# Scale rows and softmax-sum rows through DRAM, and negated maxima by ScalarE, in a two-layer contextual attention kernel

## The chip, the core and the metric

One core of one Trainium2 chip runs the whole kernel. The metric is the device time of one execution in microseconds, the median of several runs. Five engines work from queues of their own and meet by semaphores: TensorE (PE; PEld are its weight loads), VectorE (DVE), ScalarE (ACT), GpSimd (POOL) and SyncE (SP), which here only issues transfers.

## The reference

Two layers of the same operation on `b` of 4 images x 64 channels x 80 x 80. All masks are zero, so `mm` is 1. Per image:

```python
f = b[:, :, ::2, ::2]                                # 40 x 40
w = patches(f, 3, stride=1)                          # 1600 patches of 64*3*3
raw_w = patches(b, 4, stride=2)                      # 1600 patches of 64*4*4
norm = sqrt(sum(w * w))                              # one per patch
wn = w / maximum(norm, 1e-4)
yi = einsum('bpd,bld->blp', w, wn) * mm              # l scaled by its norm
yi = softmax(yi * 10, axis=1) * mm                   # over l, for each position p
out = einsum('blp,bld->bpd', yi, raw_w)              # then overlap-add of the 4x4 patches, / 4
```

The scores before scaling are symmetric in `p` and `l`; the scale belongs to one side, the softmax sum to the other.

## The kernel before

A unit is one image in one layer: 8 units. The 1600 positions are 14 tiles of 123 partitions (`TW`, 3 strips of 41). The score matrix `G` stays in SBUF, tile `t` in partitions, all positions along the free side. It is walked in four chunks of columns of 2, 4, 4 and 4 tiles for scores (`S_CHUNKS`) and 4, 4, 4 and 2 for the second half (`P_CHUNKS`), each in 7 pairs of tiles: 28 pairs, one per slot.

One loop body (L339, L526, L736, L1004, one for each engine) has 28 slots, `s` = 2 to 29. Three units are in flight in it: `u` is in its second half (softmax and products), `v` in its scores, `w` is being loaded. The order within a slot is written out by hand and is the same on all engines. First body (None, 0, 1), then six of (u, u+1, u+2), one without `w`, and a last one with `u` alone.

Scores of a pair: TensorE makes products of shifted feature tiles in `psG` (L465), or transposes blocks of `G` that exist already (L475); ScalarE copies them to `G` (L656, L672), VectorE adds a third row (L860). `maxima` (L886) multiplies a tile of `G` with the scale row `RB` and reduces the maximum to `mx`; `negate` (L902) writes `nm = -mx`; ScalarE's `score_sums` (L685) takes `Exp` with bias `nm` and accumulates the sum `sg`. In slots 23, 24, 28 and 29 four chunk sums become `lse`, in two parts: tiles 0 to 3, then the rest.

Second half of a pair: `argument_pair` (L960, VectorE, four slots ahead) computes `G * RA - lse row`; `softmax_pair` (L701, ScalarE) takes `Exp`; SyncE's `shift_pair` (L317) moves the result one partition on, SBUF to SBUF, in two transfers of 112 and of 10 rows (`SHIFT_PARTS`), to `SH`; `add_shifted` (L972, two slots ahead) adds it; `sum_pair` (L981, one slot ahead) makes `Z`, at the start of a chunk with the strip `SHJ` from `shift_strip` (L328); `paste_tile` (L509, TensorE) multiplies `Z` with the image blocks `B` into `psO`, and `read_out` (L710, ScalarE, slots 7, 14, 21, 28) copies `psO` to `OSB`, which `store_chunk` (L309) writes to DRAM.

Two vectors with one value per position are needed as rows, the same in all 123 partitions: the scale (`RB`) and `lse`. Both are made as columns, position in the partition. `spread` (L404) makes a row from a column: a transpose on TensorE whose input is one column, broadcast to 123 columns. Scale rows take 14 transposes per unit in four groups, in slots 25 and 26 (groups 0 and 1, of the unit to come), 4 (group 2) and 18 (group 3, two tiles), each followed by a ScalarE copy to `RB` (L633). Softmax rows take 14 in four chunks, in slots 24, 2, 5 and 10 (the last with two tiles); VectorE reads them in PSUM bank `k % 2` of `psB`.

SyncE's queue takes in order, per slot: feature loads (3 transfers, slot 3), image loads (6, slot 9), `shift_pair`, `shift_strip`, feature layout (slots 10 to 12), `store_chunk` (slots 8, 15, 22 and 29). It waits in front of each.

Of the kernel before, what the change touches and what calls it, by code (L numbers as in the profile page):

```python
# [28 lines left out]
NK = len(P_CHUNKS)  # L29
SLOTS = NK * PAIRS  # L30
# [11 lines left out]
FIRST = 2  # L42
# [38 lines left out]
def contextual_attention(nc, x, mask0, mask1, ident, valid, out):  # L81
    mid = nc.dram_tensor("mid", (IMAGES, C, SIDE, SIDE), F32, kind="Internal").ap()

    with ExitStack() as ctx:
# [19 lines left out]
        SQ = sb("SQ", [128, FROWS // 2 * TW], F32)  # L104
        RB = sb("RB", [TW, TILES * TW], F32)
# [22 lines left out]
        R = sb("R", [TW, TILES], F32)  # L128
# [35 lines left out]
        r_rows = sem("r_rows")  # L164
        norm_cols = sem("norm_cols")
# [33 lines left out]
        R_STEPS = 10  # L199
# [8 lines left out]

        ROW_BANK = [psB[0:TW, 1, :], psB[0:TW, 1, :], psM[0:TW, :], psB[0:TW, 0, :]]

# [52 lines left out]
        def _(sp):  # L263
# [119 lines left out]
        def _(pe):  # L383
# [4 lines left out]
            def row_squares(v, w):  # L388
                pe.wait_ge(sq_made, (w + 1) * SQ_STEPS)
                pe.sem_inc(pe_gate, 1)  # L390
                if v is not None:

                    pe.wait_ge(r_rows, v * 4 + 3)
# [16 lines left out]
            def scale_rows(u, v, g):  # L410

                pe.wait_ge(r_step, (v + 1) * R_STEPS)
                if u is not None:
                    pe.sem_inc(pe_gate, 1)
                    if g == 2:
                        pe.wait_ge(b_made, (u + 1) * PAIRS)
                    else:
                        pe.wait_ge(arg_made, u * NB + (3 if g == 3 else NK) * TILES)
                if g == 1:
                    pe.sem_inc(pe_gate, 1)  # L420
                    pe.wait_ge(r_rows, v * 4 + 1)
                spread(ROW_BANK[g], R, 4 * g, min(4 * g + 4, TILES)).then_inc(r_psum, 1)

            def lse_row(v, w, k):
# [3 lines left out]
                if k == 0:  # L428
                    pe.wait_ge(r_rows, v * 4 + 4)
                elif k == 1 and w is not None:  # L430
                    pe.wait_ge(r_rows, w * 4 + 2)
                else:
                    pe.wait_ge(arg_made, v * NB + (k - 1) * TILES)
                s0, n = P_CHUNKS[k]
                spread(psB[0:TW, k % 2, :], lse, s0, s0 + n).then_inc(lse_rows, 1)

            def block_group(v, w, g):
                if g == 0:
                    pe.wait_ge(image_in, (v + 1) * 6 * 16)
                    pe.sem_inc(pe_gate, 1)  # L440

                if g:
                    pe.wait_ge(b_made, v * PAIRS + g)
                elif w is not None:
                    pe.wait_ge(r_step, w * R_STEPS + 4)
                else:
                    pe.wait_ge(r_rows, v * 4 + 3)
# [78 lines left out]
            def body(u, v, w):  # L526
                for s in BODY:
                    at = place(u, v, s)
                    pairs = score_list(s) if v is not None else []
                    if s == 4 and v is not None:  # L530
                        scale_rows(u, v, 2)
                    if s == 18 and v is not None:
                        scale_rows(u, v, 3)
                    if s == 5 and u is not None:
                        lse_row(u, v, 2)
                    if s == 10 and u is not None:
                        lse_row(u, v, 3)
# [13 lines left out]
                    if s == FIRST and u is not None:  # L551
                        lse_row(u, v, 1)
# [8 lines left out]
                    if s == 24 and v is not None:  # L561
                        lse_row(v, w, 0)
# [24 lines left out]
            scale_rows(None, 0, 0)  # L587
            scale_rows(None, 0, 1)
# [7 lines left out]
        def _(act):  # L596
# [36 lines left out]
            def scale_rows(v, g):  # L633
                act.wait_ge(r_psum, v * 4 + g + 1)
                n = min(4, TILES - 4 * g) * TW
                act.activation(RB[:, 4 * g * TW:4 * g * TW + n], ROW_BANK[g][:, 0:n], ACT.Copy).then_inc(r_rows, 1)
# [99 lines left out]
            def body(u, v, w):  # L736
                for s in BODY:
# [29 lines left out]
                    if s == 4 and v is not None:  # L767
                        scale_rows(v, 2)
                    if s == 18 and v is not None:
                        scale_rows(v, 3)  # L770
                    if w is not None:
                        if s == 5:
                            high_features(w)
                        if s == 6:
                            squares(w)
                        if s == 12:
                            roots(w)
                        if s in (25, 26):
                            scale_rows(w, s - 25)
# [14 lines left out]
            scale_rows(0, 0)  # L794
            scale_rows(0, 1)
# [9 lines left out]
        def _(dve):  # L805
# [31 lines left out]
            def scales(v, w):  # L837
# [10 lines left out]
                if v is not None:  # L848

                    dve.sem_inc(dve_gate, 1)  # L850
                    dve.wait_ge(r_rows, (v + 1) * 4)
                mm = mm20[:, bass.ds(w * TILES, TILES)]
                dve.tensor_tensor(R[:, :], rcp[:, :], mm, ALU.mult).then_inc(r_step, 1)
# [32 lines left out]
            def maxima(v, j, par):  # L886
# [3 lines left out]
                if i == 0 and par == 0 and k != 1:  # L890
                    dve.wait_ge(r_rows, v * 4 + max(k + 1, 2))
                    dve.sem_inc(dve_gate, 1)
# [9 lines left out]
            def negate(v, j):  # L902
                dve.wait_ge(max_made, v * NB + 2 * j + 2)
                c = j // PAIRS * TILES + 2 * (j % PAIRS)
                dve.tensor_scalar(nm[:, c:c + 2], mx[:, 2 * (j % 2):2 * (j % 2) + 2], -1.0, None,  # L905
                                  ALU.mult).then_inc(neg_made, 1)

            def score_pair(v, j):

                add_third_row(v, j, 0)  # L910
                if j - 1 not in (-1, 22):
                    maxima(v, j - 1, 1)
                    negate(v, j - 1)
                add_third_row(v, j, 1)
                maxima(v, j, 0)
                if j in (22, SLOTS - 1):

                    maxima(v, j, 1)
                    negate(v, j)
# [40 lines left out]
            def argument_pair(at):  # L960
                u, k, i = at
                c0, n = p_cols(k)
                if i == 0:
                    dve.wait_ge(lse_rows, u * NK + k + 1)
                    dve.sem_inc(dve_gate, 1)
                for t in arg_tiles(i):
                    g = G[:, t * GLEN + c0:t * GLEN + c0 + n]
                    dve.scalar_tensor_tensor(out=g, in0=g, scalar=RA[:, bass.ds(u * TILES + t, 1)],  # L968
                                             in1=psB[0:TW, k % 2, 0:n],
# [34 lines left out]
            def body(u, v, w):  # L1004
                for s in BODY:
# [26 lines left out]
                    if w is not None:  # L1032
# [6 lines left out]
                        if s == 20:  # L1039
                            scales(v, w)  # L1040
# [41 lines left out]
            scales(None, 0)  # L1082
# [62 lines left out]
```

## Time and profile before

| | us |
|---|---|
| median of three runs | 1434.59 (1431.02 to 1434.99) |
| the profiled execution | 1435.39 |
| its span, first to last instruction | 1433.6 |

```profile
PEld 4756765676556665577656676567655766566433
DVE 3667889799888898889897888979987898978983
ACT 2677646676557565586565764666655855658331
```

The three lines show the span in 40 equal slices, each digit the busy share in tenths. A unit's period of about 170 us is 4.7 slices: VectorE and ScalarE are fullest together where the scores of one unit end and the second half of it begins.

```profile
L697 ACT ACTIVATE S<-S,nm 123x480 f32<-123x480 f32 (+3 forms) x560 | 308.5, 555 | 161.2 <-DVE nm L905 160.8
L968 DVE SCALAR_TENSOR_TENSOR G<-G,RA,psB 123x492 f32<-123x492 f32 (+1 forms) x448 | 270.4, 647 | 0.0
```

A group's line has: line, engine, operation, output <- inputs, shapes, count | busy us, mean ns of one | idle time of the engine in front of them, and what ended most of it.

### The profile page before, as it was taken

What the parts mean: (1) busy time and instruction counts of PE and PEld (TensorE: products, weight loads), DVE (VectorE), ACT (ScalarE), POOL (GpSimd) and SP (SyncE); (2) the same over time, 40 slices, a digit from 0 to 9 for tenths busy, and PEclk for the clock granted to TensorE, in tenths of its full rate; (3) what the DMA queues carried; (4) which work ended last, traced back from release to release, by engine and by line L of the source; (5) the groups of instructions that cost most, each with busy time, mean ns of one, the idle gap of its engine ahead of it and who ended that gap; (6) DMA issues with size and microseconds to landing.
All of it is one profiled execution on the core that took longest, in us unless ns stands there. A gap on an engine that the chain in (4) does not pass through costs nothing.

```text
span 1433.6 us, 24384 instructions
## 1 busy us (share of the span) xinstructions
PE 1327.2 (93%) x7190; PEld 894.6 (62%) x7190; DVE 1183.3 (83%) x2827; ACT 857.9 (60%) x2233; POOL 46.9 (3%) x62
## 2 busy tenths in 40 slices
PE   4988999999999899999999899999999999998886
PEld 4756765676556665577656676567655766566433
DVE  3667889799888898889897888979987898978983
ACT  2677646676557565586565764666655855658331
POOL 1000000010000100001000000001000010000100
PEclk9997999999999999999999999999999999999998
DMA  5502482145822556135741359224572236313442
GB/s 91 89 1 85 109 173 76 47 116 119 163 64 67 124 113 150 49 86 127 143 117 33 104 118 179 70 52 110 126 156 67 71 107 135 94 32 96 131 136 53
DMA packets 180471, 142.54 MB, mean 99 GB/s; under 512 B 119859, under 2 KB 177267, under 8 KB 180339
## 3 DMA queue, kind: packets, MB, share of 16 engines
q1 hardware_dynamic: 180178, 140.50, 41.7%
q8 instruction: 57, 0.93, 0.3%
q10 hardware_dynamic: 160, 0.49, 0.2%
q14 instruction: 76, 0.61, 0.1%
HBM read 19.76 MB, written 13.11 MB: 23 GB/s over the span
## 4 chain that ended last, share of the span: by engine, by line
PE 54%; DVE 15%; ACT 11%; issue 8%; SPq 7%; DMA 5%; DVEq 0%; POOL 0%; ACTq 0%; POOLq 0%
PE psO L521 26%; PE psG L471 23%; SPq L326 4%; DVE G L968 4%; ACT S L697 4%; DVE Z L1001 3%; DMA SH<-G 3%; PE psG L480 3%; DVE S L898 3%; ACT G L708 2%; ACT G L683 2%; DVE G L979 2%; DMA SHJ<-G 2%; SPq L270 1%; ACT SQ L624 1%
## 5 line engine op out<-in xcount | busy, mean ns | idle before, releaser
L521 PE MATMUL psO<-Z,B 123*128 123x492 f32 (+2 forms) x1792 | 718.6, 530 | 46.0 <-DVE Z L1001 31.4
L521 PEld LDWEIGHTS psO<-Z,B 123*128 123x128 f32 x1792 | 325.8, 194 | 247.6 <-issue 133.8
L471 PE MATMUL psG<-LH,HL 128*123 128x246 f16 (+2 forms) x2616 | 407.2, 285 | 3.7 <-ACT G L670 3.0
L697 ACT ACTIVATE S<-S,nm 123x480 f32<-123x480 f32 (+3 forms) x560 | 308.5, 555 | 161.2 <-DVE nm L905 160.8
L471 PEld LDWEIGHTS psG<-LH,HL 128*123 128x123 f16 x2616 | 277.4, 137 | 125.4 <-issue 64.5
L708 ACT ACTIVATE G<-G,nb 123x492 f32<-123x492 f32 (+1 forms) x448 | 265.0, 639 | 60.3 <-DVE G L968 59.9
L898 DVE CUSTOM_DVE_ANT_0 S<-G,RB 123x492 f32<-123x492 f32 (+1 forms) x448 | 268.4, 604 | 25.8 <-ACT G L683 15.6
L979 DVE TENSOR_TENSOR G<-G,SH 123x492 f32<-123x492 f32 (+1 forms) x448 | 247.6, 591 | 48.9 <-DMA SH<-G 48.3
L968 DVE SCALAR_TENSOR_TENSOR G<-G,RA,psB 123x492 f32<-123x492 f32 (+1 forms) x448 | 270.4, 647 | 0.0
L883 DVE TENSOR_TENSOR G<-G,psG 123x492 f32<-123x492 f32 (+2 forms) x272 | 135.0, 496 | 90.4 <-PE psG L471 46.5
L1001 DVE TENSOR_TENSOR Z<-G 123x984 f32<-123x984 f32 (+2 forms) x192 | 197.2, 1028 | 0.0
L471 PE MATMUL psG<-H 128*123 128x123 f16 (+3 forms) x872 | 193.8, 284 | 0.0
L683 ACT ACTIVATE G<-psG 123x492 f32<-123x492 f32 (+3 forms) x256 | 119.7, 471 | 117.0 <-PE psG L471 76.3
L670 ACT ACTIVATE G<-psG 123x246 f32<-123x246 f32 (+1 forms) x136 | 63.6, 468 | 115.5 <-PE psG L471 115.2
L480 PEld LDWEIGHTS psG<-idn,G 123*123 123x123 f32 x672 | 95.4, 190 | 59.0 <-issue 22.4
L480 PE MATMUL psG<-idn,G 123*123 123x123 f32 x672 | 108.5, 281 | 17.9 <-ACT G L683 13.2
L471 PEld LDWEIGHTS psG<-H 128*123 128x123 f16 x872 | 102.7, 137 | 21.0 <-issue 0.4
L471 PE MATMUL psG<-HL 128*123 128x492 f16 (+2 forms) x392 | 111.8, 285 | 0.0
L697 ACT ACTIVATION_READ_ACCUMULATOR S<-S,nm 123x1 f32 x560 | 106.7, 191 | 0.0
L1109 POOL COPY G<-G 123x246 f32<-123x246 f32 x56 | 42.9, 774 | 1292.4 <-DVE mx L898 1162.5
L717 ACT ACTIVATE OSB<-psO 128x492 f32<-128x492 f32 (+2 forms) x64 | 31.4, 548 | 78.8 <-PE psO L521 78.7
L471 PE MATMUL psG<-HV 128*123 128x246 f16 (+2 forms) x240 | 67.7, 282 | 0.0
(79 smaller groups left out, 575.8 us busy)
## 6 DMA issues: line engine op xcount, KB each, us to landing
SH<-G SPq DMA_DIRECT2D x336, 214.8 KB
SH<-G SPq DMA_DIRECT2D x112, 89.2 KB
SH<-G SPq DMA_DIRECT2D x336, 19.2 KB
XP<-x SPq DMA_DIRECT2D x20, 280.0 KB, 5.7
XP<-mid SPq DMA_DIRECT2D x20, 280.0 KB, 5.5
HL<-LH SPq DMA_DIRECT2D x16, 246.5 KB, 4.5
mid<-OSB SPq DMA_DIRECT2D x48, 80.0 KB, 2.3
out<-OSB SPq DMA_DIRECT2D x48, 80.0 KB, 2.3
```

What stands on the lines that cost most here:

```text
L471: last = pe.matmul(psG[0:TW, bank, b0 * TW:b1 * TW], st[:, v % 2, p:p + TW], mv[:, v % 2, lo:lo + n], start=i == 0, stop=i == len(terms) - 1)
L480: last = pe.transpose(psG[0:TW, par, i * TW:(i + 1) * TW], G[:, c:c + TW], idn[0:TW, 0:TW])
L521: last = pe.matmul(psO[:, b, 0:n], B[:, o:o + 128], Z[:, 2 * (s % 2) + j, 0:n], start=t == 0, stop=t == TILES - 1)
L670: act.activation(to, psG[0:TW, FREE, stored * TW:w * TW], ACT.Copy).then_inc(p_copied, 1)
L683: act.activation(G[:, c:c + n], psG[0:TW, par, 0:n], ACT.Copy).then_inc(part if shared else read, 1)
L697: last = act.activation(y, y, ACT.Exp, bias=nm[:, k * TILES + t:k * TILES + t + 1], accum_out=sg[:, c:c + 1])
L708: act.activation(y, y, ACT.Exp, bias=nb[:, bass.ds(u * TILES + t, 1)]).then_inc(y_made, 1)
L883: dve.tensor_tensor((odd if par else even)[:, b0 * TW:n], rows[:, p0 * TW:p0 * TW + n - b0 * TW], psG[0:TW, par, b0 * TW:n], ALU.add).then ...
L898: dve.tensor_tensor_reduce(S[:, slot, 0:n], tile_of(j, 2 * i + par)[:, 0:n], RB[:, s0 * TW:s0 * TW + n], 1.0, 0.0, ALU.mult, ALU.max, mx[: ...
L968: dve.scalar_tensor_tensor(out=g, in0=g, scalar=RA[:, bass.ds(u * TILES + t, 1)], in1=psB[0:TW, k % 2, 0:n], op0=ALU.mult, op1=ALU.subtrac ...
L979: dve.tensor_tensor(g, g, SH[:, o % SFREE, 0:n], ALU.add).then_inc(y1_made, 1)
L1001: dve.tensor_tensor(Z[:, slot:slot + 2, 0:n], g[:, 2 * i:2 * i + 2, c0:c0 + n], g[:, 2 * i - 1:2 * i + 1, c0 - TW:c0 - TW + n], ALU.add).t ...
```

## The change

1. Scales. Of unit 0, groups 0 and 1 are still made by `spread`. Otherwise one transpose per unit (`turn_scales`, slot 22) turns the 14 columns of `RA` into 14 rows of 123, ScalarE copies them (slot 23), SyncE writes them to DRAM (slot 24) and loads them back, broadcast to 123 partitions, one load per score chunk: slots 26 and 28 for the next unit's chunks 0 and 1, slots 4 and 10 for chunks 2 and 3. The column vector `R` goes; `RA` held the same.
2. Softmax sums. Rows of chunks 0 and 1 are made as before, each in a PSUM bank of its own. The last six tiles (chunks 2 and 3) are turned by one transpose (slot 2), copied by ScalarE (slot 2), written (slot 3) and loaded, broadcast, into `LB` (slot 5). VectorE's arguments of chunks 2 and 3 read `LB`.
3. `negate` runs on ScalarE, in front of the exponentials of its pair; that of pair 22 at the start of slot 23.

Waits are set to match. The core of the diff:

```diff
+RFIRST = 8
+LHEAD = 8
+LTAIL = TILES - LHEAD
...
+            def write_scales(w):
+                sp.wait_ge(scales_copied, w + 1)
+                sp.dma_start(scale_row[w].rearrange("(t p) -> t p", p=TW), RT[:, :]).then_inc(scales_out, 16)
+            def load_scales(w, k):
+                t0, n = S_CHUNKS[k]
+                if w == 0:
+                    if t0 + n <= RFIRST:
+                        return
+                    n, t0 = t0 + n - max(t0, RFIRST), max(t0, RFIRST)
+                else:
+                    sp.wait_ge(max_made, (w - 1) * NB + (k + 1) * TILES)
+                    sp.sem_inc(sp_gate, 1)
+                sp.wait_ge(scales_out, (w + 1) * 16)
+                row = scale_row[w:w + 1, t0 * TW:(t0 + n) * TW]
+                sp.dma_start(RB[:, t0 * TW:(t0 + n) * TW], row.to_broadcast([TW, n * TW])).then_inc(scales_in[k], 16)
+            def write_lse(u):
+                sp.wait_ge(lse_copied, u + 1)
+                sp.dma_start(lse_tail[u].rearrange("(t p) -> t p", p=TW), LT[:, :]).then_inc(lse_out, 16)
+            def load_lse(u):
+                sp.wait_ge(arg_made, u * NB)
+                sp.sem_inc(sp_gate, 1)
+                sp.wait_ge(lse_out, (u + 1) * 16)
+                sp.dma_start(LB[:, :], lse_tail[u:u + 1, :].to_broadcast([TW, LTAIL * TW])).then_inc(lse_in, 16)
...
+                    if s == FIRST and u is None:
+                        write_scales(v)
+                    if s == 3 and u is not None:
+                        write_lse(u)
+                    if s == 5 and u is not None:
+                        load_lse(u)
+                    if s in (4, 10) and v is not None:
+                        load_scales(v, 2 if s == 4 else 3)
+                    if s == 24 and w is not None:
+                        write_scales(w)
+                    if s in (26, 28) and w is not None:
+                        load_scales(w, 0 if s == 26 else 1)
...
+            def turn_scales(u, w):
...
+                pe.transpose(psB[0:TILES, 1, 0:TW], RA[:, w * TILES:(w + 1) * TILES],
+                             idn[0:TW, 0:TW]).then_inc(scales_turned, 1)
+            def turn_lse(v, u):
...
+                pe.transpose(psM[0:LTAIL, 0:TW], lse[:, LHEAD:TILES], idn[0:TW, 0:TW]).then_inc(lse_turned, 1)
...
-                    if s == 4 and v is not None:
-                        scale_rows(u, v, 2)
-                    if s == 18 and v is not None:
-                        scale_rows(u, v, 3)
-                    if s == 5 and u is not None:
-                        lse_row(u, v, 2)
-                    if s == 10 and u is not None:
-                        lse_row(u, v, 3)
...
-                        lse_row(u, v, 1)
+                        lse_row(u, 1)
+                        turn_lse(v, u)
...
+                    if s == 22 and w is not None:
+                        turn_scales(u, w)
...
-                    if w is not None and s in (25, 26):
-                        scale_rows(u, w, s - 25)
...
+                act.activation(RT[:, :], psB[0:TILES, 1, 0:TW], ACT.Copy).then_inc(scales_copied, 1)
...
+                act.activation(LT[:, :], psM[0:LTAIL, 0:TW], ACT.Copy).then_inc(lse_copied, 1)
...
+            def negate(v, j):
+                act.wait_ge(max_made, v * NB + 2 * j + 2)
+                c = j // PAIRS * TILES + 2 * (j % PAIRS)
+                act.activation(nm[:, c:c + 2], mx[:, 2 * (j % 2):2 * (j % 2) + 2], ACT.Copy,
+                               scale=-1.0).then_inc(neg_made, 1)
             def score_sums(v, j):
                 k, i = j // PAIRS, j % PAIRS
+                if j != 22:
+                    negate(v, j)
...
+                    if s == 23 and v is not None:
+                        negate(v, 22)
...
+                row = psB[0:TW, k, 0:n] if k < 2 else LB[:, c0 - LHEAD * TW:c0 - LHEAD * TW + n]
```

## Rows read from the trace of the kernel before

**Rows 1.** Page, busy time of each engine (us, share of the span, instructions).
```profile
PE 1327.2 (93%) x7190; PEld 894.6 (62%) x7190; DVE 1183.3 (83%) x2827; ACT 857.9 (60%) x2233; POOL 46.9 (3%) x62
```
**Rows 2.** Page, chain of waits, shares of the span by engine.
```profile
PE 54%; DVE 15%; ACT 11%; issue 8%; SPq 7%; DMA 5%; DVEq 0%; POOL 0%; ACTq 0%; POOLq 0%
```
**Rows 3.** List of waits, whole span: waiting us in total, times, longest.
```profile
ACT S L697 <- DVE nm L905: 160.8, 120, 4.1
...
DVE G L979 <- DMA SH<-G: 48.3, 26, 4.8
...
PE psO L521 <- DVE Z L1001: 31.4, 17, 4.6
...
PE psO L521 <- ACT OSB L717: 4.8, 6, 1.9
```
**Rows 4.** Windows of one steady unit: us, busy of each engine (instructions), clock, DMA share, GB/s.
```profile
666.40:672.40 6.00, 6.00 (x50) 4.86 (x48) 4.74 (x13) 3.63 (x10) 0.03 (x1) 1.00 1.01 218
682.00:773.00 91.00, 89.41 (x407) 53.80 (x408) 78.39 (x178) 48.46 (x119) 0.00 (x0) 1.00 0.49 109
773.00:818.00 45.00, 40.60 (x237) 30.24 (x236) 38.73 (x106) 38.34 (x116) 1.65 (x3) 1.00 0.27 73
```
**Rows 5.** Chain in order of time, TensorE, 682 to 698 us: start, us, what.
```profile
682.25 3.54 PE psO L521 x8
...
697.76 0.21 PE psB L406 x2
```
**Rows 6.** Groups by form, VectorE: count, busy us, mean ns, idle before.
```profile
L979 DVE TENSOR_TENSOR G<-G,SH 123x492 f32<-123x492 f32 x336 | 210.8, 665 | 41.5 <-DMA SH<-G 40.9
...
L883 DVE TENSOR_TENSOR G<-G,psG 123x492 f32<-123x492 f32 x128 | 85.3, 667 | 42.3 <-PE psG L471 39.7 <-ACT G L670 2.7
...
L905 DVE TENSOR_SCALAR nm<-mx 123x2 f32<-123x2 f32 x224 | 38.0, 169 | 7.8
```
**Rows 7.** Timeline of VectorE, 793 to 801 us: start, us, engine, line, operation.
```profile
793.54 0.08 DVE L898 DVE_READ_ACCUMULATOR2_ANT mx<- 123x1 f32 x1
...
793.93 0.67 DVE L898 CUSTOM_DVE_ANT_0 S<-G,RB 123x492 f32<-123x492 f32 x1
...
799.96 0.08 DVE L898 DVE_READ_ACCUMULATOR2_ANT mx<- 123x1 f32 x1
799.96 1.36 DVE L968 SCALAR_TENSOR_TENSOR G<-G,RA,psB 123x492 f32<-123x492 f32 x2
```
**Rows 8.** Timeline of ScalarE, 23 and 788 us.
```profile
23.24 0.22 ACT L629 ACTIVATE lnn<-nsq 123x14 f32<-123x14 f32 x1 [6.88 <-DVE nsq L835]
23.49 0.21 ACT L631 ACTIVATE root<-lnn 123x14 f32<-123x14 f32 x1
...
788.40 0.22 ACT L729 ACTIVATE ed<-df 123x16 f32<-123x16 f32 x1
788.51 0.56 ACT L697 ACTIVATE S<-S,nm 123x320 f32<-123x320 f32 x1
```
**Rows 9.** Timeline of SyncE's queue, 661 to 675 us.
```profile
661.74 2.07 SPq L270 DMA_DIRECT2D XP<-mid  x3
663.91 9.65 SPq L326 DMA_DIRECT2D SH<-G  x12
673.69 1.22 SPq L337 DMA_DIRECT2D SHJ<-G  x2
```
**Rows 10.** Timeline of VectorE, 670 to 679 us, with its idle time and what ended it.
```profile
670.05 0.67 DVE L979 TENSOR_TENSOR G<-G,SH 123x492 f32<-123x492 f32 x1 [0.95 <-DMA SH<-G]
...
677.65 0.67 DVE L997 TENSOR_TENSOR Z<-G,SHJ 123x492 f32<-123x492 f32 x1 [1.14 <-DMA SHJ<-G]
678.24 0.66 DVE L998 TENSOR_TENSOR Z<-G 123x492 f32<-123x492 f32 x1
```
**Rows 11.** DMA issues: count, KB each, median us to landing.
```profile
HL<-LH SPq DMA_DIRECT2D x16, 246.5 KB, 4.5
...
out<-OSB SPq DMA_DIRECT2D x8, 20.0 KB, 1.9
```

More of the change, by code:

```diff
@@ L82, in contextual_attention @@
     mid = nc.dram_tensor("mid", (IMAGES, C, SIDE, SIDE), F32, kind="Internal").ap()
+    scale_row = nc.dram_tensor("scale_row", (UNITS, TILES * TW), F32, kind="Internal").ap()
+    lse_tail = nc.dram_tensor("lse_tail", (UNITS, LTAIL * TW), F32, kind="Internal").ap()
     with ExitStack() as ctx:
@@ L104, in contextual_attention @@
         SQ = sb("SQ", [128, FROWS // 2 * TW], F32)
+        RT = sb("RT", [TILES, TW], F32)
+        LT = sb("LT", [LTAIL, TW], F32)
+        LB = sb("LB", [TW, LTAIL * TW], F32)
         RB = sb("RB", [TW, TILES * TW], F32)
@@ L164, in contextual_attention @@
         r_rows = sem("r_rows")
+        scales_turned = sem("scales_turned")
+        scales_copied = sem("scales_copied")
+        scales_out = sem("scales_out")
+        scales_in = [sem(f"scales_in{k}") for k in range(NK)]
+        lse_turned = sem("lse_turned")
+        lse_copied = sem("lse_copied")
+        lse_out = sem("lse_out")
+        lse_in = sem("lse_in")
         norm_cols = sem("norm_cols")
@@ L390, in row_squares @@
                 pe.sem_inc(pe_gate, 1)
-                if v is not None:
-                    pe.wait_ge(r_rows, v * 4 + 3)
+                if v:
+                    pe.wait_ge(b_made, v * PAIRS)
                 for r in range(FROWS // 2):
@@ L424, in lse_row, with scale_rows @@
-            def lse_row(v, w, k):
+            def scale_rows(g):
+                pe.wait_ge(r_step, R_STEPS)
+                spread(psB[0:TW, g, :], RA, 4 * g, 4 * g + 4).then_inc(r_psum, 1)
+            def turn_scales(u, w):
+                pe.wait_ge(r_step, (w + 1) * R_STEPS)
+                pe.sem_inc(pe_gate, 1)
+                if u is not None:
+                    pe.wait_ge(arg_made, u * NB + 2 * TILES)
+                else:
+                    pe.wait_ge(r_rows, 2)
+                pe.transpose(psB[0:TILES, 1, 0:TW], RA[:, w * TILES:(w + 1) * TILES],
+                             idn[0:TW, 0:TW]).then_inc(scales_turned, 1)
@@ L426, in lse_row @@
+            def turn_lse(v, u):
+                pe.wait_ge(lse_dve, (u + 1) * LSE_STEPS)
+                pe.sem_inc(pe_gate, 1)
+                pe.wait_ge(b_made, (u + 1) * PAIRS)
+                pe.transpose(psM[0:LTAIL, 0:TW], lse[:, LHEAD:TILES], idn[0:TW, 0:TW]).then_inc(lse_turned, 1)
+            def lse_row(v, k):
                 pe.wait_ge(lse_dve, v * LSE_STEPS + (LSE_STEPS // 2 if k == 0 else LSE_STEPS))
                 pe.sem_inc(pe_gate, 1)
[L428 to L431, printed above, removed]
+                if k == 1:
+                    pe.wait_ge(scales_copied, min(v + 2, UNITS))
+                elif v == 0:
+                    pe.wait_ge(r_rows, 1)
@@ L432, in lse_row @@
                 else:
-                    pe.wait_ge(arg_made, v * NB + (k - 1) * TILES)
+                    pe.wait_ge(arg_made, (v - 1) * NB + (k + 1) * TILES)
                 s0, n = P_CHUNKS[k]
-                spread(psB[0:TW, k % 2, :], lse, s0, s0 + n).then_inc(lse_rows, 1)
+                spread(psB[0:TW, k, :], lse, s0, s0 + n).then_inc(lse_rows, 1)
             def block_group(v, w, g):
@@ L445, in block_group @@
                     pe.wait_ge(r_step, w * R_STEPS + 4)
[L446 to L447 removed]
+                elif v:
+                    pe.wait_ge(b_made, v * PAIRS)
                 for t in (2 * g, 2 * g + 1):
@@ L586, in _ @@
             band_sums(None, 0)
-            scale_rows(None, 0, 0)
-            scale_rows(None, 0, 1)
+            scale_rows(0)
+            scale_rows(1)
+            turn_scales(None, 0)
             body(None, 0, 1)
@@ L766, in body @@
                         softmax_pair(at)
[L767 to L770, printed above, removed]
+                    if s == FIRST and u is not None:
+                        copy_lse(u)
                     if w is not None:
@@ L793, in _ @@
             roots(0)
-            scale_rows(0, 0)
-            scale_rows(0, 1)
+            scale_rows(0)
+            scale_rows(1)
+            copy_scales(0)
             act.wait_ge(mask_ready, 1)
@@ L835, in squared_norms, with scales @@
                 dve.tensor_scalar(nsq[:, :], psM[0:TW, 0:TILES], 1e-8, None, ALU.max).then_inc(r_step, 1)
-            def scales(v, w):
+            def scales(w):
                 at = w * R_STEPS
@@ L889, in maxima @@
                 n = w * TW
-                if i == 0 and par == 0 and k != 1:
-                    dve.wait_ge(r_rows, v * 4 + max(k + 1, 2))
+                if i == 0 and par == 0:
+                    if k < 2 and v == 0:
+                        dve.wait_ge(r_rows, 2)
+                    else:
+                        dve.wait_ge(scales_in[k], (v + k // 2) * 16)
                     dve.sem_inc(dve_gate, 1)
@@ L968, in argument_pair @@
                     dve.scalar_tensor_tensor(out=g, in0=g, scalar=RA[:, bass.ds(u * TILES + t, 1)],
-                                             in1=psB[0:TW, k % 2, 0:n],
+                                             in1=row,
                                              op0=ALU.mult, op1=ALU.subtract).then_inc(arg_made, 1)
@@ L1039, in body @@
                         if s == 20:
-                            scales(v, w)
+                            scales(w)
             dve.wait_ge(mask_step, 1)
@@ L1081, in _ @@
             squared_norms(0)
-            scales(None, 0)
+            scales(0)
             body(None, 0, 1)
```

54 lines of the change are left out of this document (21 added, 33 removed).

## The prediction

> **What bounds the kernel now.** I read the busy shares of the page first: TensorE is busy for 93% of the span, VectorE 83%, ScalarE 60% [rows 1]. Alone that says "take work off TensorE", and the change takes 136 small transposes off it. So I read the chain of waits next: only 54% of it is TensorE's; 15% is VectorE, 11% ScalarE, 7% SyncE's queue and 5% transfers [rows 2]. The reader is to see that the bound changes hands. The list of waits says where: TensorE waits 31.4 us for VectorE's sums `Z` and 4.8 us for the output copies, ScalarE 160.8 us for the negated maxima `nm`, VectorE 48.3 us for shift transfers [rows 3]. Last I cut one steady unit (654 to 824 us, a period of 170 us) into windows [rows 4] and walked the chain through it. Three stages come out.
>
> Stage one, 654 to 682 us (slots 2 to 7): TensorE is full, but a second path ends almost together with it. SyncE issues nearly without a break from 654 to 673 (store, shifts, three feature loads, shifts) [rows 9], the 16 DMA engines are saturated in 666 to 672 [rows 4], VectorE waits 0.95 us for a shift and later 1.14 us for the strip `SHJ` [rows 10], and the stage ends when ScalarE, after features and squares, has copied `OSB`: TensorE starts again at 682.25 [rows 5].
>
> Stage two, 682 to 773 us (slots 7 to 20): TensorE is busy 89.4 of 91 us [rows 4]. What leaves TensorE here counts in full.
>
> Stage three, 773 to 818 us (slots 21 to 29): ScalarE is busy 38.3 and VectorE 38.7 of 45 us [rows 4]; the chain runs on ScalarE from 781 to 790, then on VectorE until 817, where TensorE takes up a sum `Z` that it has waited for (17 such waits, up to 4.6 us [rows 3]).
>
> **The change, part by part.**
>
> *Transposes gone from TensorE.* One column-to-row transpose is 0.21 us / 2 = 0.105 us of the chain [rows 5]. A unit had 28; now it has 8 (softmax rows of chunks 0 and 1) plus two single ones that turn 14 and 6 columns at once. In stage two go those of chunk 3 in slot 10 and of scale group 3 in slot 18, 4 together: 0.42 us, off the path that ends the stage. Seven bodies have both: 2.9 us. In stage one go 8 and come 1: 0.74 us, in stage three go 8 and come 1; both lie beside the other paths.
>
> *Negation moved.* VectorE: 224 instructions of 169 ns [rows 6]. What one is worth depends on what follows. From the end-read of one maximum to the next maximum it takes 0.39 us (793.54 to 793.93), and with no negation between, the next instruction starts with the read itself (799.96) [rows 7]. So 0.39 before a maximum; before an argument I take 0.19, the instruction and its start, and before an add 0.35, an estimate between the two, nearer to the first because an add has gates to pass as a maximum has. On the path of stage three lie two of the first kind, one of the second and one of the third: -1.32 us. ScalarE: a small instruction whose result the next one needs costs 23.49 - 23.24 = 0.25 us; one that nothing right behind it needs, 788.51 - 788.40 = 0.11 us [rows 8]. Where the exponentials already waited for `nm` (most of the 160.8 us) it costs nothing: 0.17 + 0.04 us of VectorE is replaced by 0.21 + 0.04 of ScalarE. It costs in the unbroken ScalarE run 781 to 790: pairs 20 and 21 at 0.25, pair 22 (taken out in front) at 0.11: +0.61 us, which VectorE's sum of slot 23 waits for. Stage three: +0.61 - 1.32 = -0.71 us.
>
> *Row copies on ScalarE.* Four copies per unit go, two of 14x123 and 6x123 come. None of those gone lies in the run 781 to 790; they cover part of the other negations. I take 0.
>
> *Rows from SBUF in place of PSUM for the arguments of chunks 2 and 3.* The trace has no such instruction before. An add with a PSUM operand takes 667 ns, one without 665 ns [rows 6]: I take 0, bounds 0.06 us either way for each of 28 tiles. The Trainium skill (VectorE: DVE Perf Modes, The TRN2 errata) gives a fixed 58 cycles for SBUF sources against 120 for PSUM; by that the 28 instructions would save 1.8 us of VectorE a unit, most of it in stage two where VectorE is not the bound. The two rows above speak against it.
>
> *Seven more issues on SyncE.* Each takes about 0.7 us of its queue (three feature loads: 2.07 us [rows 9]). Order matters. The write of the scales (slot 24) and the loads of slots 26 and 28 fall in gaps, though the last one ends just when the shift of slot 29 wants the queue: +0.1 us at the head of SyncE's unbroken stretch. The write in slot 3 comes behind that slot's shifts, so the shift for which VectorE waits 0.95 us isn't touched. But it and the load of slot 4 push the shifts of slot 5 and the strip (issued 673.69 [rows 9]) back: 1.3 us less some 0.8 us for which SyncE stood idle in that row of twelve issues, 0.5 us. VectorE's sum ended at 678.9 and TensorE used it at 682.25, 3.3 us later [rows 10, 5]: covered. If the strip came over 3 us later, or the sum after it over 1 us, all beyond is lost. The loads of slots 5 and 10 and of the last unit's row are needed five or more slots on. No instruction of VectorE should wait for a row. Write and load together are two transfers of 2 to 4.5 us [rows 11] against 12 us between their slots.
>
> *What survives stage one.* It starts 0.71 us earlier and TensorE has 0.74 us less in it, but SyncE's stretch starts 0.1 us later, and in units where ScalarE's run to `OSB` starts right behind TensorE one negation adds 0.25. If SyncE's path decides everywhere, nothing survives; if TensorE's does, 1.2 us. TensorE has six waits at `OSB`, from nearly nothing to 1.9 us [rows 3], so both happen. I take 0.3 us, near the lower end, since a path that was second becomes first.
>
> *The sum.* Seven bodies of -0.42 - 0.3 = -5.0. First body (no shifts yet; the chain is TensorE, then ScalarE, then VectorE; two removed copies and 14 removed transposes lie on it, and +0.61 as above): -2.0, bounds -4 and +1. Last body, where VectorE and SyncE are the chain and have two issues more: +0.7, bounds 0 and +3. Together -6.3 us. The profiled execution took 1435.39 us (span 1433.6), 0.8 above the median of 1434.59; 1434.6 - 6.3 = 1428.3. I say **1428.5**.
>
> **The rivals.**
>
> *A, stage one eats it (no change).* SyncE's queue and the strip are the path in every unit, ScalarE's added 0.25 falls before `OSB`, and only the 0.42 of stage two stays, against +0.7 at the end and perhaps a short spell at the lower clock more: -2.9 + 0.7 + 0.7 = -1.5: 1433. For it: the saturated 666 to 672 and both waits in rows 10. Against: the waits there are about 1 us.
>
> *B, all of it counts (faster).* -0.42 - 1.2 a unit, and -3 at the start: -14: 1420. For it: TensorE's 93%. Against: rows 2 and 10.
>
> *C, the broadcast loads crowd out the shifts (slower).* Place: slots 4 and 5. Each load writes 123 rows of 1968 bytes (2952 for the softmax row), 242 and 363 KB. A load of 246.5 KB lands after 4.5 us, one of 20 KB after 1.9 [rows 11], so 2.6 us is moving when it is spread well. If few of the 16 engines carry it, they move the same bytes for several times 2.6 us, and the strip and shifts behind it wait for just those engines. The kernel cuts its shifts into 112 and 10 rows, so that most rows are a multiple of 16; the loads aren't cut. It decides from the point at which the strip lands over 1 us later than now (the smallest cover of the sum behind it). On 3 of 16 engines it would be 13.9 us at the moving rate of that row, of which about 4 pass before the strip is issued and 4 are covered: up to +6 a unit. That row's time holds queueing, so the lower bound is 0. I price it at +2 us a unit in seven units, with +3 at the end: 1428.5 + 14 + 3 = 1445. The Trainium skill (DMA: Bandwidth & Descriptors, Why a DMA increments its semaphore by 16 and not by 1) says that a transfer uses the largest number of engines up to 16 that divides its slowest dimension; for 123 rows that is 3. No row of before shows how many engines a transfer used.
>
> **How the numbers follow.** Forecast 0.42, A 0.22, B 0.13, C 0.23. This kernel's runs tell 0.3% (4.3 us) from no change, so faster is below 1430.3, slower above 1438.9. Faster: 0.7 of the forecast's 0.42, B, and a fifth of A: 0.29 + 0.13 + 0.04 = 0.46. Slower: nearly all of C, 0.21, and 0.01 of the rest: 0.22. Same: 0.32. Range 1419 to 1442: it takes in B and A and the lower half of C. The forecast's own range is 1424 to 1432.
>
> **What would show it.** Right: 4 transposes less per unit between the `OSB` copies of slots 7 and 21, with that stretch 0.4 us shorter; from that copy to TensorE's restart in slot 29 about 0.7 us less; TensorE's wait at `OSB` in slot 7 grown from 0.8 to about 2 us (so part is lost there). ScalarE's new negation near 0.2 us, VectorE's waits for rows 0. C would show as waits of VectorE for `SHJ` or `SH` well over the 48.3 us of rows 3, and as a bigger wait of TensorE for `Z` in slots 8 to 13. B would show no wait at `OSB`. It would be wrong if ScalarE's run in stage three grew by more than 1.3 us, or if SyncE stood waiting for a DRAM write with shifts queued behind it.

## The result

The changed kernel is slower: 1443.81 us median of 6 runs (1441.28 to 1445.91), against 1431.27 us for the kernel before, run beside it. The ratio is 1.0087, 95% interval [1.0064, 1.011]. The forecast was 1428.5 us, range 1419 to 1442, so the sign was wrong. Rival C had the sign, part of the place and, with 1445 us, nearly the time.

The profiled execution took 1445.91 us (span 1444.1), at the granted clock of before (0.983 both). Busy times and the shares of the chain of waits, from the page of after; they answer to [rows 1] and [rows 2]:

```profile
PE 1317.9 (91%) x7054; PEld 875.8 (61%) x7054; DVE 1138.6 (79%) x2595; ACT 888.5 (62%) x2443; POOL 46.8 (3%) x62
...
PE 32%; DVE 18%; SPq 14%; ACT 13%; issue 11%; DMA 10%; DVEq 0%; POOL 0%; ACTq 0%; POOLq 0%
```

The work went as the diff says: TensorE 136 instructions less, VectorE 44.7 us less. Yet the span grew by 10.5 us: TensorE's idle time (span less busy time) went from 106.4 to 126.2 us, and SyncE's queue and the transfers went from 12% of the chain to 24%. The list of waits, answering to [rows 3] (waiting us, times, longest):

```profile
ACT nm L763 <- DVE mx L981: 169.1, 116, 4.6
...
DVE G L1058 <- DMA SH<-G: 63.3, 44, 4.8
...
DVE Z L1076 <- DMA SHJ<-G: 42.4, 29, 4.2
...
PE psO L588 <- DVE Z L1080: 24.5, 17, 3.0
...
PE psG L538 <- DVE G L963: 15.6, 14, 2.3
...
PE psO L588 <- ACT OSB L800: 5.5, 5, 1.7
```

The second and third rows show what happens to VectorE: it waits 15.0 us more for shifts than in [rows 3], and 42.4 us for strips, which had been

```profile
DVE Z L997 <- DMA SHJ<-G: 18.7, 20, 3.9
```

before. The fifth row is what TensorE sees of it: it waits for adds that VectorE makes late, for which it had waited

```profile
PE psG L471 <- DVE G L883: 0.2, 1, 0.2
```

before. These waits are no measure of the loss by themselves: below stand kernels with nearly as much of them and no loss. No line has VectorE waiting for `RB` or `LB`: the new rows come in time, their neighbours don't.

Two stretches of one unit show how. SyncE's queue at the start of stage one, first of before, then of after (start, us, queue, line, transfer, count):

```profile
823.06 3.90 SPq L314 DMA_DIRECT2D mid<-OSB  x6
827.06 2.83 SPq L326 DMA_DIRECT2D SH<-G  x4
830.02 2.07 SPq L270 DMA_DIRECT2D XP<-mid  x3
```
```profile
824.00 0.36 SPq L371 DMA_DIRECT2D RB<-scale_row  x1
824.45 2.81 SPq L342 DMA_DIRECT2D SH<-G  x4
827.32 5.59 SPq L330 DMA_DIRECT2D mid<-OSB  x6
833.02 2.84 SPq L342 DMA_DIRECT2D SH<-G  x4
835.99 1.36 SPq L286 DMA_DIRECT2D XP<-mid  x2
```

Six stores take 5.59 us to issue in place of 3.90: behind the load of slot 28 the second one alone held SyncE for 2.31 us. Only part of that belongs to the three engines, as the first experiment shows. The packet records have that load's 123 rows moving from 825.0 to 830.1, three at a time. And two windows of after (window, us, busy of PE, PEld, DVE, ACT and POOL, granted clock, DMA share, GB/s):

```profile
851.00:852.00 1.00, 1.00 (x8) 0.70 (x6) 0.53 (x1) 0.97 (x3) 0.00 (x0) 1.00 0.20 77
853.00:854.00 1.00, 0.69 (x7) 0.46 (x5) 0.96 (x2) 0.97 (x4) 0.00 (x0) 1.00 0.20 80
```

A share of 0.20 is 3 of 16 engines (0.19). In the second rows of `LB` move alone; they start at 852.45. In the first, what moves is nearly all of one kind: the last 37 rows of a shift (1964 bytes each), issued behind the load of slot 4. The share says that the other engines move nothing: the shift ends on three engines. The last 17 rows of the strip's size, up to 852.4, go the same way. The timeline of VectorE in this unit (the bracket is its idle time and what ended it), answering to [rows 10]:

```profile
844.28 0.67 DVE L1058 TENSOR_TENSOR G<-G,SH 123x492 f32<-123x492 f32 x1 [1.80 <-DMA SH<-G]
...
846.28 0.67 DVE L1058 TENSOR_TENSOR G<-G,SH 123x492 f32<-123x492 f32 x1 [1.34 <-DMA SH<-G]
...
853.04 0.67 DVE L1076 TENSOR_TENSOR Z<-G,SHJ 123x492 f32<-123x492 f32 x1 [1.51 <-DMA SHJ<-G]
```

### The profile page after: what moved, and what is told of

It reads as the page before. It is cut to its first block, busy times and chain, and to the rows that moved or that the text cites. A ratio compares the mean times of both kernels' runs of the same rounds, so it can differ in the third digit from the quotient of the medians.

```text
span 1444.1 us, 24161 instructions
## 1 busy us (share of the span) xinstructions
PE 1317.9 (91%) x7054; PEld 875.8 (61%) x7054; DVE 1138.6 (79%) x2595; ACT 888.5 (62%) x2443; POOL 46.8 (3%) x62
## 4 chain that ended last, share of the span: by engine, by line
PE 32%; DVE 18%; SPq 14%; ACT 13%; issue 11%; DMA 10%; DVEq 0%; POOL 0%; ACTq 0%; POOLq 0%
PE psO L588 15%; PE psG L538 15%; SPq L342 8%; DMA SH<-G 6%; DVE G L1047 5%; ACT S L780 5%; DMA SHJ<-G 4%; DVE Z L1080 4%; ACT G L791 3%; SPq L286 3%; SPq L330 2%; DVE G L963 2%; ACT G L758 2%; DVE S L981 2%; DVE G L1058 2%
## 5 line engine op out<-in xcount | busy, mean ns | idle before, releaser
L1047 DVE SCALAR_TENSOR_TENSOR G<-G,RA,psB 123x492 f32<-123x492 f32 x224 | 151.6, 722 | 0.2
L763 ACT ACTIVATE nm<-mx 123x2 f32<-123x2 f32 x224 | 44.9, 200 | 169.9 <-DVE mx L981 169.1
L1047 DVE SCALAR_TENSOR_TENSOR G<-G,RA,LB 123x492 f32<-123x492 f32 (+1 forms) x224 | 120.1, 579 | 0.0
```

## The experiments

Each ratio is to the kernel before, run on the same chip. Intervals are of 95%. Where the time went I read from the start of TensorE's first product on `Z` in slots 2, 8 and 21 of each unit. The table has the difference to before (us) in one profiled execution each: "start" is up to slot 2 of unit 1, the stages are sums over units 1 to 6, "tail" is the rest.

```
kernel                     ratio    start  one    two    three  tail    low 1  low 3
e5  negation on ScalarE    1.0007   -0.1   +4.7   -0.4   -5.8   -1.2      3.4    3.4
after                      1.0087   -0.5   +9.9   +3.6   -4.3   +1.8      0.0   13.7
e1  loads of 128 rows      1.0007   -3.9   +13.2  -2.8   -5.7   +2.0     13.7    6.8
e10 loads of 126 rows      1.0016   -4.2   +7.9   -2.5   -6.3   -1.5      6.8    6.8
e9  loads of 127 rows      1.1089   +18.3  +68.7  +60.4  -8.8   +10.8    54.6    0.0
e2  negation on VectorE    1.0112   -1.5   +3.8   +7.9   -2.4   +1.6      0.0   13.7
e3  slot 28 of 128 rows    1.0043   -4.4   +8.6   +1.4   -6.1   +2.9      0.0    6.8
e6  slot 28 of 123 rows    1.0045   -4.8   +9.7   -3.3   -4.3   +1.5      6.8   10.2
e15 e1, loads twice        1.0003   -3.5   +7.4   -2.2   -5.7   +0.8      0.0   10.2
e7  128 rows, moved        0.9983   -3.9   +3.9   -2.4   -3.1   +1.6      3.4   10.2
e11 as e7, VectorE negates 0.9982   +1.2   -4.1   -2.6   +0.4   +1.9      0.0   17.1
e8  123 rows, moved        1.0198   -0.4   +4.5   +19.2  -6.6   +1.7      3.4    6.8
```

The last two columns are the time in stages one and three at TensorE's lower clock (1.2 GHz, granted 0.50); the kernel before has 0.0 and 17.1. Stage two repeats well between kernels. Stages one and three don't, since these spells stand at other places in each execution. A profiled execution isn't the median either: that of before took 1435.4 us, 4 above its median beside after, that of e1 was the slowest of its twelve (1438.2, median 1431.6), that of e10 stood 4.6 and that of e8 6.2 below theirs.

**The number of engines.** e1, all loads of 128 rows into tiles of 128 partitions:

```
-LB = sb("LB", [TW, LTAIL * TW], F32)
+LB = sb("LB", [128, LTAIL * TW], F32)
...
-row.to_broadcast([TW, n * TW])
+row.to_broadcast([128, n * TW])
```

> The changed kernel with both broadcast tiles of 128 partitions and loads of 128 rows in place of 123 (4% more bytes, the same number and place of transfers). Theory F (few engines: a load of 123 rows runs on 3 of the 16 DMA engines, and the stores, shifts and strip behind it wait for those three): the loss goes. VectorE's waits for SH and SHJ come back from 106 to about 70 us, no store issue stalls (2.3 us in slot 29), and the time falls by 10 to 16 us, to 0.995 to 1.000 of before. Theory I (seven more issues on SyncE, or simply 9 MB more bytes): nothing changes by more than 3 us, 1.008. Theory N (negation on ScalarE): nothing changes either, 1.008.

1431.64 us, 1.0007 [0.9991, 1.0024]. The whole loss goes, with 4% more bytes loaded. The strip's line is back at

```profile
DVE Z L1076 <- DMA SHJ<-G: 19.9, 22, 3.9
```

and 128 rows of `LB` move in 2.3 us, up to 15 at a time, where 123 rows took 5.2, three at a time. One thing was expected and didn't come: that no issue of a store stalls. The six stores above take 4.66 us in e1 (the longest 1.38). In the mean of the slot 29 stores of six bodies they take 4.19 us in before, 5.21 in after and 4.60 in e1, so 0.6 of the 1.0 us a unit is the three engines'. The other cause on trial, the negation (e2, back on VectorE in the changed kernel; e5, moved to ScalarE in the kernel before):

> The changed kernel with the sign change back on VectorE, loads of 123 rows as they were. Theory N: the loss goes, 1.000. Theories F and I: VectorE loses its gain of about 0.7 us a unit in slots 21 to 29 while the waits for shifts stay, so the time is the same or 2 to 5 us more: 1.008 to 1.012.

> The kernel before with nothing but the sign change moved to ScalarE. Theory N: slower by 8 to 12 us, 1.007. Theory F and my own sum (stage three -0.7 us a unit, part of it lost in slot 7): -1 to -4 us, 0.997 to 0.999.

e2: 1448.17 us, 1.0112 [1.0082, 1.0142]. e5: 1432.7 us, 1.0007 [0.9994, 1.002], so the gain expected of it (0.997 to 0.999) isn't there either. The negation isn't the loss. Two more kernels ask how the engines are chosen, with 126 and with 127 in place of 128:

> The change with loads of 126 rows. If the number of engines is the largest number up to 16 that divides the rows, 126 gives 14 engines: ratio 1.000 to 1.002, like the loads of 128 rows (1.0007), landing in some 4 us. Rival: only whole multiples of 16 rows are spread over all engines and any other number falls to few: ratio 1.006 or more.

> The change with loads of 127 rows, a prime. By the same rule one engine carries the whole load: 127 rows one after another at 82 to 118 ns each make 10 to 15 us a load against 3.4 to 5 us with three engines, the scale and softmax rows come late or hold one engine's share of shifts and strips: ratio 1.02 to 1.05, DMA share 0.06 in a stretch with such a load alone. Rival (the rows are spread by size and not by divisors): ratio 1.000 to 1.002, as with 128.

126 rows: 1433.38 us, 1.0016 [0.9997, 1.0035]. 127 rows: 1587.99 us, 1.1089 [1.1069, 1.1108], worse than I had expected. TensorE idles for 223.9 us of it (before 106.4), and its clock is at 1.2 GHz for 166 us (before 49). The packet records have its 127 rows of `LB` moving one after another for 15.4 us, and in a stretch with a load alone (columns as before) VectorE does nothing:

```profile
1138.00:1140.00 2.00, 2.00 (x23) 1.50 (x22) 0.00 (x0) 0.42 (x1) 0.00 (x0) 1.00 0.06 25
```

0.06 is one engine of 16. Its waits:

```profile
DVE G L1058 <- DMA SH<-G: 158.0, 48, 11.0
...
DVE Z L1076 <- DMA SHJ<-G: 85.2, 32, 8.6
```

By the Trainium skill (DMA: Bandwidth & Descriptors, Why a DMA increments its semaphore by 16 and not by 1) the number of engines is the largest up to 16 that divides the slowest dimension: 16 for 128 rows, 14 for 126, 3 for 123, 1 for 127. The runs agree: 3 and 1 are read from the DMA shares (0.20 and 0.06), and 126 rows cost no more than 128 within the intervals, which rules out that only multiples of 16 are spread. No row tells 14 engines from 16 (126 rows of `LB` move in 2.6 us in the same unit).

**Which load.** e3: only slot 28's load has 128 rows; e6: only slot 28's keeps 123.

```
+rows = 128 if w and k == 1 else TW        # e3; e6: "if not (w and k == 1)", LB of 128 rows
+sp.dma_start(RB[0:rows, ...], row.to_broadcast([rows, n * TW]))
```

> The changed kernel with only the load of slot 28 (scale rows of chunk 1, 242 KB) at 128 rows; the loads of slots 4, 5, 10 and 26 keep 123. Theory F, if the stalled store behind the slot 28 load starts the loss (SyncE's queue held up 1.7 us): half or more of the loss goes, 1.002 to 1.005. If the loads of slots 4, 5 and 10 do it (strip and shifts behind them): under a quarter goes, 1.007. Theories I and N: 1.008.

> The change with all loads of 128 rows but slot 28's, which keeps 123: the converse of the kernel in which slot 28's alone had 128 (1.0043 against the change's 1.0087). If the costs of the loads add, this one shows the half that slot 28 carries: ratio 1.004 to 1.006 (1.0007 and 0.0044). If slot 28's load on three engines hurts only together with the later ones: 1.001 to 1.003.

e3: 1438.14 us, 1.0043 [1.0029, 1.0058]. e6: 1436.99 us, 1.0045 [1.003, 1.0059]. The costs add: 0.0044 goes by spreading it (1.0087 - 1.0043), 0.0038 comes by narrowing it (1.0045 - 1.0007). One load a unit, which I had priced at 0.1 us, carries near half of the loss, some 6 us: the one right in front of the stores. How it does so is shown only in part. The slot 29 stores take 5.20 us in e6 against 4.60 in e1, and 4.86 in e3 against 5.21 in after, 0.4 to 0.6 us a unit. VectorE's waits for shifts and strips don't follow this load: together they are 106.9 us in e3 and 105.7 in after, 72.9 in e6 and 73.5 in e1. That they alone don't make the time is also seen in e15 below, with 90.5 us of them and no loss.

**Where the loads stand.** e7 (128 rows) and e8 (123 rows) take four transfers out of stage one:

```
-if s == 3 and u is not None: write_lse(u)
-if s == 5 and u is not None: load_lse(u)
-if s in (4, 10) and v is not None: ...
-if s in (26, 28) and w is not None:
+if s == 6 and u is not None: write_lse(u)
+if s == 8 and u is not None: load_lse(u)
+if s in (10, 13) and v is not None: ...
+if s in (26, 27) and w is not None:
```

> The change with loads of 128 rows as in the kernel of full rows (ratio to before 1.0007), and with the four transfers that it had put into stage one's busy queue moved: slot 28's scale load to slot 27, the write and the load of the softmax rows from slots 3 and 5 to slots 6 and 8, slot 4's scale load to slot 13. Theory Q (stage one is bound by SyncE's queue and by the transfers behind it; the added issues hold up the shifts by about 1.3 us a unit and what stages two and three gain, 0.7 to 1.1 us a unit, is eaten there): slots 6 to 9 lose nothing, ratio 0.993 to 0.997, 1421 to 1426 us, and VectorE's waits for SH and SHJ go back to what before had (48 and 19 us). Rival V (stages two and three gave nothing, the moved sign change and the shorter TensorE work only move idle time about): ratio 0.999 to 1.002.

> The same moves of the four transfers, but with the loads of 123 rows of the change. Theory F (a load of 123 rows goes through 3 of 16 DMA engines and hurts what is queued behind it on those three): away from stage one's stores and strip little waits behind them, so most of the loss goes: ratio 0.997 to 1.002, and a stretch with such a load alone shows a DMA share near 0.19. Rival P (a load on few engines costs the same wherever it stands, since every slot has shifts behind it): ratio 1.006 to 1.010, as the change itself.

e7: 1429.58 us, 0.9983 [0.997, 0.9996]: faster than before and than the change, but than before by 2 us and not by the 5 to 10 expected. e8: 1460.02 us, 1.0198 [1.0182, 1.0214]: worse than the change itself, against both theories put up before it ran. Its table row puts the loss into stage two, and VectorE's timeline and list of waits say at what:

```profile
1050.48 1.37 DVE L1047 SCALAR_TENSOR_TENSOR G<-G,RA,LB 123x492 f32<-123x492 f32 x2 [4.07 <-DMA LB<-lse_tail]
```
```profile
DVE G L1047 <- DMA LB<-lse_tail: 24.2, 8, 4.9
```

The arguments of chunk 2 are made in slot 10, so my move left the load of `LB` two slots. Spread over 16 engines it makes that (e7 waited 1.5 us once); on three it doesn't. e12 gives e8's `LB` alone its 128 rows:

> The moved transfers with the softmax rows' load of 128 rows and the scale rows' loads still of 123. With both of 123 the ratio was 1.0198 and VectorE waited 24.2 us for LB; with both of 128 it was 0.9983. Theory D (the loss of that kernel is the softmax load on three engines, which arrives after the VectorE work that needs it, two slots behind its issue): nearly all of it goes, ratio 1.000 to 1.004, the wait for LB under 3 us. Theory P (each load on three engines costs the same through the shifts queued behind it, four scale loads against one softmax load a unit): most of it stays, ratio 1.012 to 1.017.

1432.52 us, 1.0009 [0.9996, 1.0022], the wait for `LB` 0.7 us. Theory D holds: four narrow scale loads, placed one slot further from the stores and later than the strip, cost 0.0026 over e7.

**Where the forecast gain went.** With the engines right, 0 to 0.2% is left of the 0.4% forecast. Is it SyncE's issues (e13: the kernel before with four more tiny stores a unit), the bytes (e15: e1 with each load issued twice), or the negation (e11: e7 with it back on VectorE)?

```
+if s in (3, 4, 5, 28) and u is not None:                                # e13
+    sp.dma_start(spare[4 * u + (3, 4, 5, 28).index(s)], idn[0:16, 0:16])
...
+sp.dma_start(TWICE[:, 0:n * TW], row.to_broadcast([128, n * TW]))       # e15
```

> The kernel before with nothing but four more small stores a unit issued by SyncE (16 x 16 floats to a spare tensor, in slots 3, 4, 5 and 28), some 0.5 us of queue each and hardly any data. Theory Q (SyncE's queue in stage one is on the path, and added issue time there holds up the shifts): 1 to 2 us a unit, ratio 1.004 to 1.009. Rival B (what costs in stage one is the data of the added loads, not their issues): ratio 0.999 to 1.002.

> The change with loads of 128 rows (ratio 1.0007), in which each load of scale and softmax rows is issued a second time, into a spare tile: 5 more loads a unit, 1.35 MB, at the same places. Theory B (the bytes of the loads, spread over all 16 engines, lengthen stage one, which is why the removed work brought nothing): the second copy costs what the first did, by the forecast's -6 us without them some 6 to 7 us, ratio 1.004 to 1.006. Rival R (evenly spread loads are all but free, and stage one gives the removed work back by itself, by what it waits for and by TensorE's clock): ratio 0.9995 to 1.002.

> The moved transfers with loads of 128 rows (ratio 0.9983), and the sign change of the maxima back on VectorE. The prediction's step (0.71 us a unit in stage three saved by the move to ScalarE) would give ratio 1.001 to 1.003 here. The rival that stage one gives every gain of the sign change back, as the kernel before with only that change has it (1.0007): ratio 0.997 to 1.000.

e13: 1432.38 us, 1.0011 [0.9998, 1.0024]. e15: 1432.16 us, 1.0003 [0.9992, 1.0013]. e11: 1429.02 us, 0.9982 [0.9969, 0.9995]. None of the three costs what was missing. Evenly spread loads are all but free even when doubled, four issues a unit cost 1.6 us (0.0011, with no cost inside the interval), and with evenly spread loads it makes no measurable difference which engine negates.

The traces say where the gain went. At the full clock TensorE's work is 13 to 15 us less in e1, e7 and e10 than in before (an estimate: busy time less half of what was busy at 1.2 GHz; 136 transposes at 0.105 us are 14.3). But its idle time is 119.7, 116.9 and 115.5 us in place of 106.4, and most of that rise lies in stage one: 14.4, 11.1 and 12.8 us over six units, where before has 5.0. It waits there for the copies of `OSB` (9.4, 8.1 and 9.2 us, before 4.6) and for late adds (5.0, 2.9 and 3.4, before none). So TensorE comes earlier and waits longer, in effect rival A. What does stand is TensorE's time in stage two. e16 tries its weight: e7 with the 16 small products of the row squares made twice in slot 8.

```
-for r in range(FROWS // 2):
+for r in list(range(FROWS // 2)) * 2:      # but once for the first unit
```

> The kernel with moved loads of 128 rows (ratio 0.9983), in which TensorE does the 16 small products of the row squares (0.108 us each) twice in slot 8, at the head of stage two: 1.7 us more a unit, 12 us over 7 bodies. Theory T (stage two is TensorE's and its work counts one for one, so the four transposes taken from it were really worth their 0.42 us): ratio 1.0057 to 1.0075. Theory G (the stages before and behind it take back what changes there, as they took back the forecast gain): ratio 1.001 to 1.004.

1450.81 us, 1.0132 [1.0107, 1.0158]: 21 us over e7 where 12 were added, beyond both theories. The added 1.7 us shows in slot 8 of each of the six units between the first and the last two one for one (8.3 us in place of 6.6 where the clock stays up). The rest comes at the end of slot 8 and in slot 9, where in five of these six units TensorE's clock falls to 1.2 GHz (0.50) for 3.4 us, once for 6.8; e7 has no such spell there. In e16 the fall comes during the 32 small products of slot 8 or right behind them. Two windows of e16 (columns as before):

```profile
1044.80:1048.30 3.50, 3.50 (x34) 3.50 (x34) 3.05 (x6) 0.00 (x0) 0.00 (x0) 1.00 0.72 172
1048.40:1051.80 3.40, 3.40 (x7) 1.52 (x7) 2.55 (x8) 1.76 (x3) 0.00 (x0) 0.51 0.74 140
```

The trace counts TensorE busy for all of the first one, with products of two columns nearly throughout, and the clock falls behind them.

A fall of the clock explains half of e1's loss in stage one, too. TensorE's slot 7 of unit 5, in before and in e1:

```profile
1021.00:1025.80 4.80, 4.80 (x22) 2.96 (x23) 4.68 (x13) 3.50 (x12) 0.00 (x0) 1.00 0.25 70
```
```profile
1022.00:1028.50 6.50, 6.50 (x22) 3.54 (x23) 6.48 (x15) 4.30 (x16) 0.00 (x0) 0.74 0.25 74
```

The same 22 products take 6.5 us at a mean granted clock of 0.74 and 4.8 us at 1.00, after a wait for `OSB` with which slot 6 ended in both. e1 had four such spells at slot 7 (1.7 us each, 6.8 of its +13.2); before had none there, e7 one. In the four units with a spell TensorE had also idled 0.6 to 1.5 us in slot 5, for late adds; in e1's other two units it hadn't. Over the whole execution the clock costs all three about the same: 49.0, 52.4 and 45.5 us at 1.2 GHz in before, e1 and e7.

## Why the prediction was wrong

*The step that failed* is "Seven more issues on SyncE". It priced each transfer by the issue time on SyncE, called slot 28's load "+0.1 us", and the delay of the strip "covered". A transfer also holds the DMA engines it runs on, and what stands behind it on them. On three engines the loads cost 0.8% (after against e1), 11 us; with engines evenly used the step would have been about right: e13's four issues and e15's doubled loads cost 1.6 us or less. Slot 28's load holds three engines for 5 us and carries near half of the loss. The stores behind it are part of the way (0.4 to 0.6 us of 0.8 to 0.9 a unit); the rest of the way is open.

*Rival C* was that mechanism, at 1445 us against 1443.81 measured. That the numbers agree is in part luck: it added 17 us to a gain of 6 and to a kernel before of 1434.6 us, where 11 us, next to no gain and 1431.3 us were measured; and it took 13.9 us for 242 KB on three engines where 5.0 was measured (825.0 to 830.1). Its place was half right: it named slots 4 and 5 and missed slot 28. It had 0.23, and against it stood that "No row of before shows how many engines a transfer used". That was a reason to ask for it before any other number: 123 was in the diff, the rule was quoted beside it, the kernel itself cut its shifts into 112 and 10 rows, and nothing in the trace spoke against it. The range was cut off at C's lower half, which is why it missed by 1.8 us.

*Transposes gone:* right. Predicted -0.42 us a unit in stage two, -2.5 over six units; e1 -2.8, e10 -2.5, e7 -2.4, e11 -2.6. In the change itself the stage is 3.6 us longer: TensorE waits in it 1.9 us for late adds (0.2 in before) and 10.4 for ScalarE's copies of `G` (8.0).

*Negation moved:* the gain of 0.71 us a unit in stage three isn't there. On ScalarE it is 200 ns as said,

```profile
L763 ACT ACTIVATE nm<-mx 123x2 f32<-123x2 f32 x224 | 44.9, 200 | 169.9 <-DVE mx L981 169.1
```

and stage three of e5's profiled execution is 5.8 us shorter over six units, which looks like 1.0 us a unit. But before spends 17.1 us of its stage three at 1.2 GHz and e5 3.4, and with half of TensorE's busy time in these spells taken off (an estimate: 7.9 and 1.5 us) stage three is 269.0 us in before and 269.6 in e5. In the two other pairs ScalarE's negation gains 0.6 us (e7 against e11) and 1.9 us (after against e2) over six units in the same way. And TensorE idles longer in stage one in all three pairs, by 3.1, 4.9 and 6.4 us. e5 can't be told from before, nor e7 from e11. So "What survives stage one", 0.3 us a unit, was too much, and so was what it should survive from; 0 fits.

*Rows from SBUF in place of PSUM:* taken as 0, and so it is. Groups by form of VectorE (count, busy us, mean ns):

```profile
L1047 DVE SCALAR_TENSOR_TENSOR G<-G,RA,psB 123x492 f32<-123x492 f32 x224 | 151.6, 722 | 0.2
L1047 DVE SCALAR_TENSOR_TENSOR G<-G,RA,LB 123x492 f32<-123x492 f32 x112 | 76.8, 729 | 0.0
```

The 1.8 us a unit that were estimated from the Trainium skill's cycles (VectorE: DVE Perf Modes, The TRN2 errata: 58 fixed ones from SBUF, 120 from PSUM) aren't there: 729 ns from SBUF, 722 from PSUM.

*Rival A*, at 1433 us, is what is left when the engines are right: e1 1431.64, e10 1433.38. Stage two's 0.42 stays, and stage one eats the rest.

*Open:* how slot 28's load makes its whole cost, and why ScalarE's copies of `OSB` don't come earlier when everything before them does; nothing was run that separates ScalarE's own work from what it waits for. That e7 beats e1 by 0.24% because less stands in SyncE's queue in stage one is what it was built on, but e13 makes the queue worth 0.1% only, and the intervals of e7 and e1 overlap.

## What to carry to other kernels

Before pricing a transfer, look at the slowest dimension of its access pattern: in these runs the largest number up to 16 that divides it was how many DMA engines carried it (3 for 123 rows, 1 for 127). Round it up to a multiple of 16, even if that moves more bytes (128 rows for 123 took 0.8% off this kernel). And price a transfer by what stands behind it on its engines; when a row for that is missing and the shape speaks for trouble, the range must hold the trouble whole.

## What was not expected of the hardware

- A narrow load can hold not only its engines but the queue that issues: the same 1328 issues take SyncE 1012 us in e9 (loads on one engine) and 892 in e10 (126 rows), and one shift issued behind slot 28's load took 3.68 us in e9 where the others took 0.5 to 0.8. Short stalls aren't proof of a narrow load, though: a store took 1.4 us behind a load of 128 rows, and 1.5 in before with no such load at all.
- One transfer on one engine (127 rows, 15.4 us) made a kernel of 1431 us 11% slower with 38 loads in it: about 4 us each. TensorE idled 118 us more than in before, and its clock stood at 1.2 GHz for 118 us more.
- The end of an evenly spread transfer shows whom it waits for: behind the load of slot 4 the last 37 rows of a shift moved at a DMA share of 0.20, three engines of 16.
- 16 products of two columns more, 1.7 us, were followed in five of six units by 3.4 us or more at half clock (0.50) and so cost about twice their time: 21 us in all for 12 us of added work.
